# A fused attention and mixture-of-experts layer on one core: the experts' gate and up products in three passes of split numbers

## The reference

```python
g = jnp.einsum('ech,ehf->ecf', buf, w_gate)
u = jnp.einsum('ech,ehf->ecf', buf, w_up)
y = jnp.einsum('ecf,efh->ech', jax.nn.silu(g) * u, w_down)
out_tok = y.reshape(E * C, H)[jnp.clip(slot, 0, E * C - 1)]
out_tok = jnp.where(accepted[:, None], out_tok * gate[:, None], 0.0)
return (xt + out_tok).reshape(B, S, H)
```

## Time and profile before

| | us |
|---|---|
| median of 3 runs (lowest, highest) | 2441.88 (2440.73, 2442.39) |
| the profiled execution | 2441.89 |
| its span, from first to last instruction | 2440.1 |
| of it before the first product of the experts | 2184.6 |
| from there to the end | 255.5 |

### The profile page before, as it was taken

How to read it: one execution, slowest core, us unless ns; L and a number is a source line. 1 busy time by engine, 2 the same in 40 slices (tenths; PEclk the granted TensorE clock), 3 DMA queues, 4 the chain that set the end, 5 groups by cost and what they waited for, 6 DMA issues and landing times.

```text
span 2440.1 us, 36843 instructions
## 1 busy us (share of the span) xinstructions
PE 2319.8 (95%) x11528; PEld 1509.0 (62%) x11528; DVE 1517.1 (62%) x4450; ACT 1041.7 (43%) x2048; POOL 1715.3 (70%) x1774
## 2 busy tenths in 40 slices
PE   6999999999999999999999999999999999849996
PEld 5565576556655666567655765566656665537774
DVE  4677656765576657765776567656766577225553
ACT  3454435543455445443544354534554454112222
POOL 0688767986788667975797669867886679524444
PEclk8999999999999999999999999999999999969998
DMA  3222200200011001100020002100110011234552
GB/s 89 62 65 62 62 10 19 65 24 18 14 44 49 14 14 36 53 19 14 19 73 21 10 19 61 27 18 14 44 49 14 14 33 41 67 110 150 183 184 67
DMA packets 96819, 118.97 MB, mean 49 GB/s; under 512 B 12288, under 2 KB 75782, under 8 KB 96624
## 3 DMA queue, kind: packets, MB, share of 16 engines
q1 hardware_dynamic: 89712, 99.98, 14.9%
q0 software_dynamic: 6912, 16.64, 2.0%
HBM read 46.91 MB, written 37.90 MB: 35 GB/s over the span
## 4 chain that ended last, share of the span: by engine, by line
PE 83%; DVE 7%; issue 4%; POOL 3%; ACT 2%; DMA 0%; SPq 0%; DVEq 0%; POOLq 0%; ACTq 0%
PE value_ps L765 20%; PE misc_ps L787 9%; PE turned_ps L742 9%; PE turned_ps L745 9%; PE misc_ps L664 8%; PE row_ps L717 7%; PE turned_ps L938 6%; PE turned_ps L717 3%; PE misc_ps L777 2%; DVE rinv L1209 1%; PE value_ps L957 1%; PE misc_ps L957 1%; POOL half_sums L516 1%; DVE masked_row L1175 1%; PE misc_ps L813 1%
## 5 line engine op out<-in xcount | busy, mean ns | idle before, releaser
L1011 ACT ACTIVATE probs<-turned_ps 128x512 f32<-128x512 f32 (+2 forms) x1280 | 647.7, 555 | 779.6 <-PE turned_ps L745 749.1
L516 POOL TENSOR_TENSOR half_sums<-half_sums,probs 128x1024 f32<-128x1024 f32 (+3 forms) x512 | 832.2, 1625 | 30.0 <-ACT probs L1011 14.1
L765 PE MATMUL value_ps<-probs,lat_keys 128*64 128x512 f32 (+3 forms) x3072 | 589.1, 505 | 2.2 <-POOL probs L491 2.2
L742 PE MATMUL turned_ps<-q_hl,lat_hi 128*128 128x512 f32 (+2 forms) x1280 | 500.2, 393 | 1.5 <-ACT fold_v L1064 1.5
L745 PE MATMUL turned_ps<-q_max,lat_lo 65*128 65x512 f32 (+2 forms) x1280 | 480.4, 375 | 1.8 <-DMA q_max<-both_rows 1.8
L491 POOL TENSOR_SCALAR_AFFINE_SELECT probs<-probs 128x256 f32<-128x256 f32 x512 | 210.6, 411 | 354.6 <-ACT probs L1011 352.0
L1175 DVE CUSTOM_DVE_ANT_0 masked_row<-row_ps,future 128x512 bf16<-128x512 f32 (+4 forms) x707 | 344.7, 508 | 136.5 <-PE row_ps L717 130.4
L765 PEld LDWEIGHTS value_ps<-probs,lat_keys 128*64 128x64 f32 x3072 | 188.2, 137 | 278.0 <-issue 211.6
L511 POOL TENSOR_TENSOR half_sums<-probs 128x768 f32<-128x768 f32 (+1 forms) x128 | 269.6, 2106 | 118.7 <-ACT probs L1011 118.6
L717 PE MATMUL row_ps<-lat_hi,q_hl 128*128 128x512 f32 (+4 forms) x1026 | 340.6, 373 | 4.9 <-DVE neg_max L1175 4.0
L717 PEld LDWEIGHTS row_ps<-lat_hi,q_hl 128*128 128x128 f32 x1026 | 189.6, 191 | 150.7 <-issue 69.7
(11 more groups left out here) (195 smaller groups left out, 2728.2 us busy)
## 6 DMA issues: line engine op xcount, KB each, us to landing
q_max<-q_hl SPq DMA_DIRECT2D x256, 128.0 KB
slots_x<-router SPq DMA_DIRECT2D x8, 1290.0 KB, 5.9
ex_x<-slots_x SPq DMA_DIRECT2D x64, 129.0 KB, 2.3
x_in<-in_L_attn_x_bld SPq DMA_DIRECT2D x8, 1024.0 KB, 5.6
layer_out<-x_in SPq DMA_DIRECT2D x8, 1024.0 KB, 4.5
ex_w<-in_L_ffn_w_gate SPq DMA_DIRECT2D x32, 256.0 KB, 3.7
ex_w<-in_L_ffn_w_up SPq DMA_DIRECT2D x32, 256.0 KB, 3.8
ex_w<-in_L_ffn_w_down SPq DMA_DIRECT2D x32, 256.0 KB, 4.4
```

The lines of the kernel that those rows point to most:

```text
L516: nc.gpsimd.tensor_tensor(total, total, now[:, :, q0:BANK], ALU.add).then_inc(added, 1)
L742: nc.tensor.matmul(scores_of(n, h), lat_hi[b % 2][:, keys], q_hl[gp % 2][:, heads, cols], start=True, stop=False)
L765: mm = nc.tensor.matmul(value_ps[h * LD:(h + 1) * LD, q0:BANK], lat_keys[b % 2][:, j, :], probs[:, n % NPROBS, h, q0:BANK], start=(j == 0) ...
L1011: nc.scalar.activation(probs[:, n % NPROBS, heads, q0:BANK], scores_of(n, h), ACT.Exp).then_inc(exp_done, 1)
```

## The change

It makes the experts' gate and up products in three passes of F32R numbers, six instructions where four stood: high weights with high rows, low weights with high rows, high weights with low rows. The parts are made new: ACT rounds the gate and up weights of an expert (`high_weights`, one instruction of 128x1024) and the transposed rows (`high_rows`, two instructions an expert), POOL subtracts to get the low weights (`low_weights`, one instruction of 128x1024 an expert), DVE subtracts to get the low rows (in `copy_rows`, in place of the two copies). Four experts' split weights are held (`NWH`). Three experts' weights (not five) are loaded early, and split in slots 7, 9 and 11 of the last pair of heads (ACT) and after its `roots` (POOL). `normalise_out(g)` on ACT moves from behind the first to behind the second expert of the next group, and the statistics of a group (now `row_statistics`) from the end of `add_to_rows` to behind `hidden` of the next group's first expert. Finished rows have four buffers (`NOUT`), and weights are loaded once the down products of the group that used the buffer are done, rows once that group is sent. Some attention buffers change place in memory (not shown).

```diff
@@ SP
             for e in range(AHEAD, E):
                 g = (e - AHEAD) // 2
-                sp.wait_ge(ex_sent[g % 2], 16 * NY * (g // 2 + 1))
-                load_rows(e)
+                sp.wait_ge(ex_y_full, NY * (g + 1))
                 load_weights(e)
+                if e % 2:
+                    sp.wait_ge(ex_sent[g % NOUT], 16 * NY * (g // NOUT + 1))
+                    load_rows(e - 1)
+                    load_rows(e)
@@ POOL
+            def low_weights(e):
+                pool.wait_ge(ex_wh_done, e + 1)
+                nc.gpsimd.tensor_tensor(ex_wl[e % NWH][:, :, :, :], ex_w[e % AHEAD][:, 0:2],
+                                        ex_wh[e % NWH][:, :, :, :].bitcast(F32), ALU.subtract).then_inc(ex_wl_done, 1)
+
+            for e in range(EARLY_W):
+                low_weights(e)
             destinations(LAST)
...
+            low_weights(EARLY_W)
             for g in range(E // 2):
+                for e in (2 * g + NWH, 2 * g + NWH + 1):
+                    if e < E:
+                        low_weights(e)
                 root(g)
                 send_back(g)
@@ PE
                 pe.wait_ge(ex_t_ready, e + 1)
+                pe.wait_ge(ex_wl_done, e + 1)
+                wh, wl = ex_wh[e % NWH], ex_wl[e % NWH]
+                passes = [(w, x, kd) for w, x in ((wh, ex_xh), (wl, ex_xh), (wh, ex_xl)) for kd in range(KD)]
...
-                        for kd in range(KD):
-                            mm = nc.tensor.matmul(turned_ps[f][:, m, 0:C], ex_w[e % AHEAD][:, m, kd, f * P:(f + 1) * P],
-                                                  ex_xT[:, g % 2, kd, u * C:(u + 1) * C],
-                                                  start=(kd == 0), stop=(kd == KD - 1))
+                        for n, (w, x, kd) in enumerate(passes):
+                            mm = nc.tensor.matmul(turned_ps[f][:, m, 0:C], w[:, m, kd, f * P:(f + 1) * P],
+                                                  x[:, g % 2, kd, u * C:(u + 1) * C],
+                                                  start=(n == 0), stop=(n == len(passes) - 1))
@@ ACT
+            def high_weights(e):
+                k = e % AHEAD
+                act.wait_ge(ex_w_loaded[k], 48 * (e // AHEAD + 1))
+                nc.scalar.copy(ex_wh[e % NWH][:, :, :, :], ex_w[k][:, 0:2]).then_inc(ex_wh_done, 1)
...
+            for u in range(2):
+                high_rows(u)
+            for e in range(EARLY_W, NWH):
+                high_weights(e)
             for e in range(0, E, 2):
                 for u in range(2):
                     activate(e + u)
-                    if e and u == 0:
+                    if e + u + 2 < E:
+                        high_rows(e + u + 2)
+                    if e and u == 1:
                         normalise_out(e // 2 - 1)
+                    if e + u + NWH < E:
+                        high_weights(e + u + NWH)
             normalise_out(E // 2 - 1)
@@ DVE
-                nc.vector.tensor_copy(ex_xT[:, g % 2, 0, cols], ex_ring[0][:, 0:width])
-                nc.vector.tensor_copy(ex_xT[:, g % 2, 1, cols], ex_ring[1][:, 0:width]).then_inc(ex_t_ready, 1)
+                for kd in range(KD):
+                    dve.wait_ge(ex_xh_done, KD * e + kd + 1)
+                    low = nc.vector.tensor_tensor(ex_xl[:, g % 2, kd, cols], ex_ring[kd][:, 0:width],
+                                                  ex_xh[:, g % 2, kd, cols].bitcast(F32), ALU.subtract)
+                low.then_inc(ex_t_ready, 1)
...
             for e in range(0, E, 2):
                 for u in range(2):
                     hidden(e + u)
+
+                    if e and u == 0:
+                        row_statistics(e // 2 - 1)
                     if e + u + 2 < E:
                         copy_rows(e + u + 2)
                 add_to_rows(e // 2)
+            row_statistics(E // 2 - 1)
```

More of the change, by code:

```diff
@@ L111, in build_layer @@
         fold_lo = sb("fold_lo", [P, KD, NPAIR * P], F32R, attn)
+        lat_hi, lat_lo = [sb("lat_hi0", [P, L], F32R, attn)], [sb("lat_lo0", [LD + 1, L], F32R, attn)]
+        lat_keys, q_hl = [sb("lat_keys0", [P, NT, LD], F32, attn)], [sb("q_hl0", [P, 2, L], F32R, attn)]
         future = sb("future", [P, BANK], F32, attn)
@@ L118, in build_layer @@
         expert_i = sb("expert_i", [P, E], I32, attn)
[L119 to L122, removed]
+        lat_hi.append(sb("lat_hi1", [P, L], F32R, attn))
+        lat_lo.append(sb("lat_lo1", [LD + 1, L], F32R, attn))
+        lat_keys.append(sb("lat_keys1", [P, NT, LD], F32, attn))
+        q_hl.append(sb("q_hl1", [P, 2, L], F32R, attn))
         fold_v = sb("fold_v", [P, NPAIR, D], F32, attn)
@@ L175, in build_layer @@
         tail = ExitStack()
-        EARLY_W = 5
+        NWH = 4
+        ex_wh = [sb(f"ex_wh{k}", [P, 2, 2, D], F32R, tail) for k in range(NWH)]
+        ex_wl = [sb(f"ex_wl{k}", [P, 2, 2, D], F32R, tail) for k in range(NWH)]
+        EARLY_W = 3
+        EARLY_SPLIT = (7, 9, 11)
         ex_w = [sb(f"ex_w{k}", [P, 3, 2, D], F32, tail) for k in range(AHEAD)]
@@ L182, in build_layer @@
         ex_x = sb("ex_x", [P, AHEAD // 2, NY, W], F32, tail)
-        ex_xT = sb("ex_xT", [P, 2, KD, 2 * C], F32, tail)
+        ex_xh = sb("ex_xh", [P, 2, KD, 2 * C], F32R, tail)
+        ex_xl = sb("ex_xl", [P, 2, KD, 2 * C], F32R, tail)
         ex_s = sb("ex_s", [P, 4, KF, C], F32, tail)
         ex_h = sb("ex_h", [P, 4, KF, C], F32, tail)
-        ex_y = sb("ex_y", [P, 2, NY, D], F32, tail)
+        NOUT = 4
+        ex_y = sb("ex_y", [P, NOUT, NY, D], F32, tail)
         neg_mean = sb("neg_mean", [P, 2 * NY], F32, tail)
@@ L241, in build_layer @@
         ex_loaded = [sem(f"ex_loaded{i}") for i in range(AHEAD)]
+        ex_w_loaded = [sem(f"ex_w_loaded{i}") for i in range(AHEAD)]
+        ex_wh_done = sem("ex_wh_done")
+        ex_wl_done = sem("ex_wl_done")
+        ex_xh_done = sem("ex_xh_done")
         ex_t_full = sem("ex_t_full")
@@ L416, in load_weights @@
                     sp.dma_start(ex_w[k][:, m], w[e].rearrange("(k p) f -> p k f", p=P)
-                                 ).then_inc(ex_loaded[k], 16)
+                                 ).then_inc(ex_w_loaded[k], 16)
             def load_rows(e):
@@ L447, in _ @@
                 g = (e - AHEAD) // 2
-                sp.wait_ge(ex_sent[g % 2], 16 * NY * (g // 2 + 1))
-                load_rows(e)
+                sp.wait_ge(ex_y_full, NY * (g + 1))
                 load_weights(e)
-            for k in range(2):
-                sp.wait_ge(ex_sent[k], 16 * NY * (E // 4))
+                if e % 2:
+                    sp.wait_ge(ex_sent[g % NOUT], 16 * NY * (g // NOUT + 1))
+                    load_rows(e - 1)
+                    load_rows(e)
+            for k in range(NOUT):
+                sp.wait_ge(ex_sent[k], 16 * NY * (E // 2 // NOUT))
         @block.gpsimd
@@ L920, in transpose_rows @@
                     for k in (e % AHEAD, e % AHEAD + 1):
-                        pe.wait_ge(ex_loaded[k], (e // AHEAD + 1) * (16 * (3 + NB)))
+                        pe.wait_ge(ex_loaded[k], (e // AHEAD + 1) * 16 * NB)
                 if e:
@@ L1084, in _ @@
                         gate_exponentials(b - 1)
+                    if gp == PAIRS - 1 and t in EARLY_SPLIT:
+                        high_weights(EARLY_SPLIT.index(t))
             copy_heads(PAIRS - 1, 1)
@@ L1096, in activate, with high_rows @@
                     nc.scalar.activation(ex_s[:, e % 4, f, :], turned_ps[f][:, 0, 0:C], ACT.Silu).then_inc(ex_s_ready, 1)
+            def high_rows(e):
+                act.wait_ge(ex_t_full, e + 1)
+                g, u = divmod(e, 2)
+                cols = slice(C + TAIL, 2 * C) if u else slice(0, C + TAIL)
+                width = 2 * P if u else C + TAIL
+                for kd in range(KD):
+                    nc.scalar.copy(ex_xh[:, g % 2, kd, cols], ex_ring[kd][:, 0:width]).then_inc(ex_xh_done, 1)
             def normalise_out(g):
@@ L1101, in normalise_out @@
                     k = g % 2 * NY + n
-                    last = nc.scalar.activation(ex_y[:, g % 2, n, :], ex_y[:, g % 2, n, :], ACT.Identity,
+                    last = nc.scalar.activation(ex_y[:, g % NOUT, n, :], ex_y[:, g % NOUT, n, :], ACT.Identity,
                                                 bias=shift[:, k:k + 1], scale=rstd[:, k:k + 1])
                 last.then_inc(ex_o_ready, 1)
+            for u in range(2):
+                high_rows(u)
+            for e in range(EARLY_W, NWH):
+                high_weights(e)
             for e in range(0, E, 2):
@@ L1382, in add_to_rows @@
                 part = slice(g % 2 * NY, (g % 2 + 1) * NY)
-                if g >= 2:
-                    dve.wait_ge(ex_sent[g % 2], 16 * NY * (g // 2))
+                if g >= NOUT:
+                    dve.wait_ge(ex_sent[g % NOUT], 16 * NY * (g // NOUT))
                 for n in range(NY):
@@ L1388, in add_to_rows, with row_statistics @@
                     dve.wait_ge(ex_y_full, g * NY + n + 1)
```

(6 more changed lines are left out.)

4 lines of the change are left out of this document (2 added, 2 removed).

## The result

The changed kernel takes 2462.44 us, the median of 4 runs (2460.23 to 2463.70), beside 2441.31 us for the kernel before, also 4 runs: a ratio of 1.0086, 95% interval 1.0070 to 1.0102. It is 21 us slower; the forecast was 25 us slower (2467). The profiled execution took 2462.42 us for a span of 2460.7. One execution of the run e9 took 4002.67 us, at a mean granted clock of 0.744, and is in no ratio.

A forecast was written before the change was run, and what follows sets the result against it. PE bounds the kernel before; afterwards POOL's 16.55 us round does. Root(0) at 2208, plus 215.2 for 13 rounds and 35.4 for the rest, gives 2458.6, a span of 2465.4 and 2467 us; range 2452 to 2480, chance 0.80.

The forecast's parts named there:

- The bound and the round: Expert stage: POOL's chain of 11.8 us plus two subtractions of 2.38 makes a round of 16.55 us, setting the pace.
- The row of the same shape: POOL's low weights: a subtraction priced at 2.38 us from a 128x1024 two-input instruction in the trace.
- the lower bound of 1.6: Rival, POOL's subtraction at 1.6 us, from a one-input copy of 256 columns four times: 2447 us; chance 0.06.
- PE's group: Expert stage: gate and up 7.2, transposes 1.1, `down` 4.74, with some 0.4 for the rows: 13.4 us.
- the longer way of the rows: Ahead of the second transposes: later statistics on DVE push the low rows back, up to 0.4 us in PE's group.
- PE's idle time: Expert stage: PE, going at POOL's pace, idles about 3.2 us a group, mostly ahead of gate and up.
- The start: Start of expert stage: first product at 2185.1, silu after the fourth weights at 2191.3, root(0) at about 2208.
- the old wait of 15.43: Before the expert stage: three early subtractions, 7.1 us, fit into POOL's 15.43 us wait for the router and cost nothing.
- The sum: Expert stage to end: 2208 + 215.2 + 35.4 = 2458.6 for the last transfer's issue; span 2465.4, time 2467 us.
- PE stays the bound: Rival, expert stage: if subtractions took little or fell into POOL's hole, rounds are 13.4 us, time 2425; chance 0.07.
- The clock's fall: Rival, expert stage: idle PE drops to the low clock for half of each group, 20 us a group, 2524; chance 0.07.

The follow-up runs named there:

- e9: The filled hole kernel with statistics and normalisation back at their places of before; 2438.29 us, ratio 0.9985 to the kernel before.
- the filled hole: The changed kernel with `root(g)` moved ahead of POOL's two subtractions, so they run while ACT normalises; 2423.78 us, ratio 0.9928 to the kernel before.

## Why the prediction was right

*The bound and the round.* Right, by the two runs that remove or double the subtraction and by the one that hides it. POOL's groups of after by shape, with count, busy us, mean ns and idle before:

```profile
L621 POOL TENSOR_TENSOR ex_wl<-ex_w,ex_wh 128x1024 fp32r<-128x1024 f32 x29 | 68.1, 2376 | 17.8 <-ACT ex_wh L1102 17.7
```

2376 ns for the predicted 2380. The row of the same shape was the right price, and the lower bound of 1.6, from a copy, was not near. The Trainium skill's figure for two inputs (GPSIMD Engine Reference, "Performance versus the Vector engine"), 2.2 us for this shape as an estimate, is 7% low again.

*PE's group.* Predicted 13.4, measured 13.23 where it shows (the run without subtractions). The 24 products take 3.53 to 3.72 us, predicted 3.6; the 0.4 us for the longer way of the rows is not there. In after it mattered to nobody. PE's idle time there, predicted at some 3.2 us a round, is 2.4 (ten rounds, above): the products themselves take 14.2 us a round instead of 13.2, at a mean granted clock of 0.94 instead of 1.00.

*The start.* POOL's and ACT's rows of after where the stage begins:

```profile
2140.64 1.04 POOL L562 TENSOR_TENSOR alone<-alone,minus_half 128x4 f32<-128x4 f32 x1
2141.66 6.96 POOL L621 TENSOR_TENSOR ex_wl<-ex_w,ex_wh 128x1024 fp32r<-128x1024 f32 x3
2157.12 0.26 POOL L568 TENSOR_SCALAR rt<-rt 128x8 f32<-128x8 f32 x1 [8.50 <-DVE rt L1354]
...
2183.01 1.04 ACT L1102 CAST ex_wh<-ex_w 128x1024 fp32r<-128x1024 f32 x1 [0.96 <-DMA ex_w<-in_L_ffn_w_down]
2184.07 1.28 ACT L1135 ACT_TABLE_LOAD   x1
2185.36 0.44 ACT L1135 ACTIVATE ex_s<-turned_ps 128x320 f32<-128x320 f32 x1
...
2202.76 0.25 POOL L637 TENSOR_SCALAR neg_mean<-mean_var 128x5 f32<-128x5 f32 x1 [7.66 <-DVE mean_var L1462]
```

Three early subtractions and what is left of the router's wait, 6.96 + 8.50, are the old wait of 15.43: hidden, as predicted. ACT waits for the fourth weights, rounds them and loads its table in the predicted order. But the silu comes 1.5 us sooner, counted from POOL's last step of attention, PE does not wait for it, where some 2 us were predicted, and the first expert takes 5.2 us (predicted 4.7). From the end of POOL's last step (2141.68) to `root(0)` are 61.1 us; predicted were 2208 - 2146.1 = 61.9.

*The sum.* `root(13)` begins at 2418.31, 215.55 us after `root(0)` (predicted 215.2), and the last transfer's issue ends at 2453.8, 35.5 us later (35.4); the span ends 6.9 behind it (6.8).

*The 4.6 us between 2467 and 2462.4.* POOL's last step before the stage begins at 2140.64, and at 2145.08 in the execution of before: 4.4 us, which no step of the prediction speaks of. By ACT's steps, 2.2 of them are there at its first exponential (51.68 against 53.91), where both kernels do the same work; such spread is in the other executions too (51.8 to 54.4). Of these 2.2, 1.5 are one group of 64 small products of PE, 7.09 us in before (from 19.44) and 5.55 in after (from 18.86): the granted clock has fallen to 0.50 in before from 20 to 24 us, and is 0.57 in after. Till 1957 the lead grows to 3.1, which was not followed up. Another 1.5 us come near 1960, ahead of any work of the change: ACT's `x1T` begins 3.1 us earlier than before (1954.45, 1957.53), the exponentials behind it 4.6 us earlier (1964.21, 1968.84). This second step is in seven of the nine profiled executions with the change (not in the filled hole or the doubled subtraction) and in none of the three with float32 products. It is PE's clock again: behind the 32 small products of the router (L813 in before, L842 in after) PE works at 0.50 from 1962 to 1968 in before, and at 0.63 in the mean from 1958.6 to 1963.2 in after; the eight `value_ps` products there take 3.25 us in the five executions without the step and 2.3 to 2.9 in the seven with it. Why the clock is back sooner in those seven, and whether the change has to do with it, stays open. The rest of the sum is off by 0.8 at the start against some 0.6 in rounds and end.

*The rivals.* That PE stays the bound was priced at 2425; with the hole filled, and without subtractions, the runs gave 2423.8 and 2424.1. Its mechanism was right, and its condition was not met in after. The clock's fall happened in part: behind the idle 3.22 us PE worked at 0.50 of the full clock, 1.2 GHz, for some 5 us, with pairs of products that show as 0.73 instead of 0.46 us, and the round stayed at 16.58. It came off PE's own idle time, as the prediction had it.

*Not foreseen.* The prediction took the moves of statistics and normalisation as part of the new pace and gave them 0.4 us. That without them a loop of 14.6 us closes, so that they are the condition for 13.2, only the run with the filled hole and the old places showed.

## What to carry to other kernels

Read an engine with a low busy share by its chain from first to last step of a round: a hole in that chain is lost to it as long as its program has nothing to put there, and work set ahead of the chain adds its full duration to the round, while the same work in the hole costs only what is longer than it (2.4 us against 0.7 each here, on POOL's own chain). When one bound is taken away, look for a loop through several engines, none of them full, before you call a moved step harmless: the two moves cost 3 us at the end by themselves and gave some 14 us once the pace allowed. Price an instruction by a row of its own shape and engine.

## What the runs showed of the hardware

The preparation of an indirect transfer can run beside POOL's tensor work. Ahead of the first transfer of a group stand 0.8 us after ACT is done; with the subtraction in front, 0.17 us are left of it, and two subtractions still take 4.68 us. In the chain of waits POOL's queue is at work on the transfers (POOLq L649, from 2304.27) while the second subtraction lasts till 2305.74. It is 0.6 us off a round, which the forecast for this run had left open (0 to 0.8). Where the transfer waits for POOL's own last step nothing is hidden: the first transfer to `slots_x` in after begins 0.79 us behind `send_idx`.

With 28 subtractions on DVE the third of POOL's five transfers in a group takes 1.16 to 1.21 us instead of 0.97, in 13 of the 14 groups from 2200 to 2400 us; the mean of all is 1042 ns, beside 1003 in the run with the filled hole. One of the 13, with DVE's subtraction:

```profile
2294.36 1.21 DVE L1468 TENSOR_TENSOR ex_wl<-ex_w,ex_wh 128x1024 fp32r<-128x1024 f32 x1
```

```profile
2295.23 1.19 POOL L650 DMA_INDIRECT layer_out<-ex_y,ex_x  x1 [0.30 <-issue]
```

In all 13 the lengthened transfer begins while a subtraction of DVE runs and overlaps its last 0.31 to 0.36 us, and in the fourteenth group no subtraction is near and no transfer is longer. The transfer ahead of it, during which the subtraction begins, keeps its 0.97 or 0.98 us. So the two go together in every group; why was not tried.
